# Latent attention: up-projection in two 128-row products per head pair, partner rows by a VectorE shuffle, another step order

## The reference

```python
c_q = _rmsnorm(x @ w_q_down.T, q_norm_w)                       # 192
q = (c_q @ w_q_up.T).reshape(b, t, H, 128 + 64)
q_nope, q_rope = q[..., :128], q[..., 128:]
kv = x @ w_kv_down.T
c_kv, k_rope_raw = kv[..., :64], kv[..., 64:]                   # one key rope for all heads
q_rope, k_rope = _apply_rope(q_rope, ...), _apply_rope(k_rope_raw, ...)
kv_up = (_rmsnorm(c_kv, kv_norm_w) @ w_kv_up.T).reshape(b, t, H, 128 + 128)
scores = q_full . k_full / sqrt(192), causal mask, softmax, @ v, @ w_o.T
```

## Time and profile before

| what | value |
|---|---|
| runs, us | 4121.14, 4110.23, 4107.7 (median 4110.23) |
| profiled execution, span | 4117.8 us |
| TensorE (PE) busy | 3583.7 us, 87% of the span |
| VectorE (DVE) busy | 3057.9 us, 74% |
| ScalarE (ACT) busy | 1939.7 us, 47% |
| GpSimd (POOL) busy | 1167.6 us, 28% |
| mean granted TensorE clock | 0.928 of 2.4 GHz |

### The profile page before, as it was taken

The page is one execution under the profiler, slowest core; times in us unless marked ns, Lnnn a source line. Parts: engine busy times, 40 slices in busy tenths (PEclk is TensorE's granted clock), DMA queues, the critical chain, the costliest instruction groups (busy, mean ns, idle before and its releaser), DMA issues. The chain is left out here.

```text
span 4117.8 us, 65960 instructions
## 1 busy us (share of the span) xinstructions
PE 3583.7 (87%) x23747; PEld 2223.2 (54%) x23762; DVE 3057.9 (74%) x6508; ACT 1939.7 (47%) x4746; POOL 1167.6 (28%) x1208
## 2 busy tenths in 40 slices
PE   7799999998981777879999979888999999997885
PEld 3466666665661345645455545465655656564543
DVE  7788988988658675543455657868988898885678
ACT  4466666665532333311333324435656656563445
POOL 2533213334302000000111122114656555553210
PEclk9899999999995888889899988999999999997877
DMA  2222222222200100020000000022212211221000
GB/s 70 65 66 67 60 62 65 66 56 56 61 14 31 34 1 24 2 76 1 22 1 1 1 31 2 27 92 83 77 68 77 72 72 72 67 79 63 2 1 21
DMA packets 240594, 185.94 MB, mean 45 GB/s; under 512 B 117648, under 2 KB 216592, under 8 KB 239184
## 3 DMA queue, kind: packets, MB, share of 16 engines
q1 hardware_dynamic: 240272, 181.73, 14.7%
HBM read 166.45 MB, written 15.20 MB: 44 GB/s over the span
## 5 line engine op out<-in xcount | busy, mean ns | idle before, releaser
L310 PE MATMUL ps<-xT,min 128*128 128x512 f32 (+1 forms) x1072 | 503.0, 614 | 30.7 <-DVE macc L3349 30.3
L3349 DVE SCALAR_TENSOR_TENSOR macc<-ps,mcw,macc 128x508 f32<-128x508 f32 (+2 forms) x408 | 302.1, 741 | 81.2 <-ACT macc L3276 71.3
L3431 POOL TENSOR_TENSOR mSQ<-mSQ,mtn 128x512 f32<-128x512 f32 x128 | 240.2, 1877 | 362.1 <-ACT mtn L3301 362.0
L310 PEld LDWEIGHTS ps<-xT,min 128*128 128x128 f32 (+1 forms) x1072 | 191.9, 191 | 250.6 <-issue 204.3
L3424 POOL TENSOR_TENSOR mE<-mE,mCB 128x1024 f32<-128x1024 f32 x128 | 302.3, 2362 | 44.5 <-DVE mE L3359 26.5
L3359 DVE TENSOR_TENSOR_SCAN mE<-mE,mid 128x1024 f32<-128x1024 f32 x128 | 296.9, 2319 | 0.0
L3209 PE MATMUL ps<-mwo,macc 128*128 128x256 f32 x1024 | 244.5, 382 | 5.4 <-DVE macc L3366 5.3
L2937 ACT ACTIVATE hE<-ps 128x512 f32<-128x512 f32 x256 | 139.0, 595 | 223.5 <-PE ps L2899 223.5
L2351 POOL TENSOR_TENSOR lP<-lP,lm 128x512 f32<-128x512 f32 x64 | 66.6, 1041 | 574.5 <-DVE lm L2324 574.5
L3297 ACT ACTIVATE mtn<-ps,mcol 128x64 f32<-128x64 f32 x1024 | 222.9, 334 | 2.9 <-PE ps L3188 2.8
L826 POOL TENSOR_TENSOR dTB<-did,dNB 128x1024 f32<-128x1024 f32 (+1 forms) x10 | 28.7, 2869 | 662.6 <-DMA dNB<-d_N 598.4
(11 more groups left out here) (581 smaller groups left out, 8470.9 us busy)
## 6 DMA issues: line engine op xcount, KB each, us to landing
mE<-m_decay SPq DMA_DIRECT2D x128, 512.0 KB, 3.6
dwk<-in_L_attn_Wk SPq DMA_DIRECT2D x64, 128.0 KB, 2.3
dwq<-in_L_attn_Wq SPq DMA_DIRECT2D x64, 128.0 KB, 2.4
dwv<-in_L_attn_Wv SPq DMA_DIRECT2D x64, 128.0 KB, 2.4
dwg<-in_L_attn_Wg SPq DMA_DIRECT2D x64, 128.0 KB, 2.4
dwo<-in_L_attn_Wo SPq DMA_DIRECT2D x64, 128.0 KB, 2.6
min<-in_m_in SPq DMA_DIRECT2D x2, 4096.0 KB, 18.5
d_N<-dNT SPq DMA_DIRECT2D x256, 16.0 KB, 1.5
```

The lines of the kernel that those rows point to most:

```text
L310: t = pe.matmul(out, w[:, j, :], self.c.xT[:, j, blk(g, 512)], start=j == 0, stop=j == 1)
L3349: x = dve.scalar_tensor_tensor(out=acc[:, :, 3 - j:T], in0=p[:, :, 0:T - 3 + j], scalar=self.cw[:, i, j:j + 1], in1=acc[:, :, 3 - j:T], op ...
L3431: pool.tensor_tensor(self.SQ[g % 2][:, :], self.SQ[g % 2][:, :], self.tn[s][:, :], ALU.add).then_inc(*self.sqa.up)
```

## The change

Per pair there is one step `q` in place of `sw` and two `q`: the swapped rotary rows of both heads into bank 2 (matrix qr, what sw_ was) and the latent rows of both heads, second head first, into bank 3 (matrix ql, which step `a` fills). The plain rotary rows are not multiplied any more; VectorE takes them from the swapped ones in bank 2, by a shuffle that exchanges neighbouring partitions (into QC), multiplies bank 2 with the sines (into QS), later QC with the cosines (step `rope`), and adds both into QA for each head. The second chunk of c_q, 64 rows, stands twice in CQ, on partitions 0-63 and 64-127 (CN has 64 columns more for it, one more scaling per 128 tokens; tr1 turns 128 rows), so that the 64-row product of bank 3 reads other rows of the array than that of bank 2. The reciprocals are a step of their own (`rc`), and the order of the list changes. M2 is written by `o` alone. Two loads of the q matrix go, two of a column of norm weights come.

```diff
-            for step, u, e in (("sw", a, 0), ("t", c, 0), ("s", b, 0), ("q", a, 0), ("t", c, 1), ("s", b, 1), ("q", a, 1), ("o", c, 0),
-                               ("acc", d, 0), ("close", d, 0), ("stats", t - 4, 0), ("rsqrt", t - 5, 0), ("scale", t - 6, 0)):
+            for step, u, e in (("s", b, 0), ("rc", c, 1), ("t", c, 0), ("q", a, 0), ("s", b, 1), ("rc", b, 0), ("t", c, 1), ("rope", a, 0),
+                               ("acc", d, 0), ("o", c, 0), ("close", d, 0), ("stats", t - 4, 0), ("rsqrt", t - 5, 0), ("scale", t - 6, 0)):
...
-    TURNS = ((0, 128), (128, 64), (192, 128))
+    TURNS = ((0, 128), (128, 128), (256, 128))
+    PARTNER = [p ^ 1 for p in range(32)]
...
-            elif step in ("sw", "q"):
-                n, b = (0, 2) if step == "sw" else (e + 1, 3)
-                pe.wait_ge(*room[b])
...
-                for i, K in enumerate((128, 64)):
-                    w = self.sw_[0:K, i, blk(pr)] if n == 0 else self.q[0:K, i, 2 * pr + e, :]
-                    t = pe.matmul(bank(b), w, self.CQ[gs][0:K, i, :], start=i == 0, stop=i == 1)
-                t.then_inc(*self.up.up)
-                room[b] = self.m2.at(u + 1) if n == 0 else self.qa.at(2 * u + e + 1)
+                pe.wait_ge(*room[2])
+                pe.matmul(bank(2), self.qr[:, 0, blk(pr)], self.CQ[gs][:, 0, :], start=True, stop=False)
+                pe.wait_ge(*room[3])
+                pe.matmul(bank(3), self.ql[:, 0, pr, :], self.CQ[gs][:, 0, :], start=True, stop=False)
+                pe.matmul(bank(2), self.qr[0:64, 1, blk(pr)], self.CQ[gs][0:64, 1, :], start=False, stop=True)
+                pe.matmul(bank(3), self.ql[64:128, 1, pr, :], self.CQ[gs][64:128, 1, :], start=False, stop=True).then_inc(*self.up.up)
+                room[2], room[3] = self.m2.at(u + 1), self.lat.at(2 * u + 2)
             elif step == "s":
...
                 pe.wait_ge(*self.qa.at(2 * u + e + 1))
+                pe.wait_ge(*self.lat.at(2 * u + e + 1))
...
-                    for r in (192, 256):
+                dve.tensor_scalar(CN[:, b, 192:256], p[:, 256 * j + 128:256 * j + 192], sn[:, b:b + 1], None, ALU.mult)
+                    for r in (256, 320):
...
-            elif step == "sw":
-                dve.wait_ge(*self.up.at(3 * u + 1))
...
-                dve.tensor_tensor(g4(self.M2[s][:, :]), g4(bank(2)), bc(self.cs[:, 1, :], 4), ALU.mult).then_inc(*self.m2.up)
-            elif step == "q":
...
-                then(dve.tensor_tensor(g4(self.QA[s][rot, e, :]), g4(bank(3)[rot, :]), bc(self.cs[rot, 0, :], 4), ALU.mult))
-                dve.wait_ge(*self.lat.at(2 * u + e + 1))
-                dve.tensor_tensor(self.QA[s][rot, e, :], self.QA[s][rot, e, :], self.M2[s][rot, :], ALU.add).then_inc(*self.qa.up)
+            elif step == "q":
+                dve.wait_ge(*self.up.at(u + 1))
+                if u:
+                    dve.wait_ge(*self.qa.at(2 * u))
+                dve.stream_shuffle(self.QC[:, :], bank(2), self.PARTNER).then_inc(*self.swapped.up)
+                dve.tensor_tensor(g4(self.QS[:, :]), g4(bank(2)), bc(self.cs[:, 1, :], 4), ALU.mult).then_inc(*self.m2.up)
+            elif step == "rope":
+                dve.wait_ge(*self.swapped.at(u + 1))
+                dve.tensor_tensor(g4(self.QC[:, :]), g4(self.QC[:, :]), bc(self.cs[:, 0, :], 4), ALU.mult).then_inc(*self.turned.up)
...
+                for e in range(2):
+                    rot = blk(e, 64)
+                    dve.tensor_tensor(self.QA[s][rot, e, :], self.QC[rot, :], self.QS[rot, :], ALU.add).then_inc(*self.qa.up)
...
+            elif step == "rc":
+                me = self.m[s][:, e, :]
                 dve.wait_ge(*self.ex.at(2 * u + e + 1))
```

More of the change, by code:

```diff
@@ L2109, in tensor @@
                 n, i = divmod(g, 2)
[L2110 removed]
+                rows = slice(64 * i, 128)
                 pe.wait_ge(*room[g])
                 for h in range(8):
[L2113 removed]
+                    t = pe.matmul(bank(g)[rows, blk(h, 64)], self.qT[:, 8 * n + h, 128 * i:192 if i else 128], self.kvT[:, 8 * n + h, 0, :],
                                   start=True, stop=True)
@@ L2184, in tensor @@
                     for x in range(2):
-                        t = pe.matmul(bank(5)[blk(x, 64), blk(j)], self.CN[gs][:, j, 192:256], self.PT[s][:, x, blk(j)], start=True, stop=True)
+                        t = pe.matmul(bank(5)[blk(x, 64), blk(j)], self.CN[gs][:, j, 256:320], self.PT[s][:, x, blk(j)], start=True, stop=True)
                 t.then_inc(*self.o.up)
@@ L2213, in scalar @@
                 n, i = divmod(g, 2)
-                rows = 64 if i else 128
+                rows = slice(64 * i, 128)
                 act.wait_ge(*self.am.at(g + 1))
-                act.copy(self.q[0:rows, i, 8 * n:8 * n + 8, :].rearrange("p (q e) n -> p q (e n)", e=2)[:, :, 64:192],
-                         bank(g)[0:rows, :].rearrange("p (q n) -> p q n", n=128)).then_inc(*self.ac.up)
+                to = self.ql[rows, i, 4 * n:4 * n + 4, :]
+                of = bank(g)[rows, :].rearrange("p (q e n) -> p q e n", e=2, n=64)
+                act.copy(to[:, :, 64:128], of[:, :, 0, :])
+                act.copy(to[:, :, 0:64], of[:, :, 1, :]).then_inc(*self.ac.up)
             elif step == "b":
@@ L2243, in scalar @@
                 if i < 2:
-                    x = act.activation(self.CQ[gs][0:n, i, :], bank(6)[0:n, :], ACT.Copy, scale=self.nw[0:n, i:i + 1])
+                    x = act.activation(self.CQ[gs][0:n, i, :], bank(6)[0:n, :], ACT.Copy, scale=self.nw1[:, 1:2] if i else self.nw[:, 0:1])
                 else:
@@ L2249, in scalar @@
             elif step == "q":
-                lat = slice(64 - 64 * e, 128 - 64 * e)
-                act.wait_ge(*self.up.at(3 * u + e + 2))
+                act.wait_ge(*self.up.at(u + 1))
                 if u >= 4:
-                    act.wait_ge(*self.sc.at(2 * u - 8 + e + 1))
-                act.copy(self.QA[s][lat, e, :], bank(3)[lat, :]).then_inc(*self.lat.up)
+                    act.wait_ge(*self.sc.at(2 * u - 6))
+                for e in range(2):
+                    lat = slice(64 - 64 * e, 128 - 64 * e)
+                    act.copy(self.QA[s][lat, e, :], bank(3)[lat, :]).then_inc(*self.lat.up)
             elif step == "s":
@@ L2347, in gpsimd @@
         for step, g, u, e in self.order():
-            if step == "s":
+            if step == "rc":
                 pool.wait_ge(*self.rc.at(2 * u + e + 1))
```

44 lines of the change are left out of this document (21 added, 23 removed).

## The result

| | before | after |
|---|---|---|
| median, us (lowest to highest, 4 runs each) | 4108.97 (4097.44 to 4121.14) | 3992.29 (3980.23 to 3998.22) |
| ratio, 95% interval | | 0.9704 (0.9678 to 0.9731) |
| span of the profiled execution, us | 4117.8 | 3996.4 |
| the stage, us | 508.1 | 385.5 |
| everything else of the span, us | 3609.7 | 3610.9 |

The change makes the kernel faster by 116.7 us in the medians and by 121.4 in the profiled executions. It takes 122.6 us less; the rest of the program is the same within 1.2.

What follows compares the result with a forecast made beforehand. TensorE bounded the pairs (12.2 of 13.13 us); afterwards a TensorE-VectorE ring. Start to 1987.3, thirty periods of 9.17 (275.1) and shared 50 give 2312.4 against 2430.2; with tail -1.5, 119 us less: 3991, range 3970 to 4030.

Steps and rivals of the forecast that it cites:

- The products: TensorE per head pair: packed 64-row passes take two slots of 0.57, q 2.85, total work 8.90 us instead of 12.2.
- Rival A: The 64-row passes of q don't pack: the ring grows by 1.14 us per pair, 36 in all, so 4027; chance 0.15.
- three slots: 64-row passes in strict program order, only the middle two side by side: 0.57 x 32 = 18 us more, 4009.
- The ring: Loop through TensorE and VectorE: sums read at 4.39, next scores at 9.17; period 9.17 us, TensorE waiting 0.27.
- Rival B: VectorE's shuffle and permutation load are dearer: 0.7 us more per pair in the ring, 22 in all, 4013; chance 0.13.
- The collision with GpSimd: VectorE's SBUF cosine product overlaps GpSimd's normalisation of P: about 0.7 us lost per microsecond of overlap, so 0.69 + 0.40.
- dn: Down-projection step, three times in the loop: scores 8.7 us late plus 2.5 for the lowered clock, 11.2 each.
- Shared steps: Steps inside the loop (dn, tr, r, close, stats, rsqrt, scale): 16.7 us together, three times, 50.
- The start: Stage's beginning: 0.94 us later from four more scalings; second pair 10.5 us at the lower clock, reaching 1987.3.
- The tail: After the last pair's scores: the same chain with one small reordering, 1.5 us less.
- Rival C: VectorE's chain keeps TensorE at the lower clock in the loop: 250 us more, 4240, slower than before; chance 0.04.
- Rival D: Stalls are cheaper: period 8.97 without permutation cost and no clock loss after dn, -6 - 8, 3977; chance 0.05.

Runs made afterwards that it cites:

- cosine-early kernel: The changed kernel with the cosine product directly behind the sine product in step q instead of in step rope: 3987.25 us, stage 382.6.
- the last experiment: The changed kernel with VectorE's part of dn behind t(c,0) and the sixteen dn scalings moved to ScalarE: 3978.1 us, stage 370.0.

## Why the prediction held, step by step

The stage lost 122.6 us, forecast 119. That the medians lie within 1.3 us of the 3991 is closer than single runs of one kernel (3980.23 to 3998.22) allow, and so partly luck; the stage and its parts are the test.

**The products: right, a little cheap.** The 64-row passes start together in banks 2 and 3, and a slot of two is 0.53 (2252.57 to 2253.10) where I had 0.57; q is 2.87 for 2.85. With t at 0.43 for 0.50, TensorE's work is 8.82 us (9.15 less 0.33) for 8.90. Rival A, unpacked, is excluded by the rows and by the kernel that has it so, whose stage is 18.1 us longer and not 36. The Trainium skill (TensorE: Matmul & The Clock Gate, Packing small matmuls) has matmuls start and end strictly in program order; here the passes in the order high, low, high, low run as two pairs, so the three slots that I had worked out from it did not come. The rows don't show in which order the two of a pair start.

**The ring: right in place and length, two of its terms wrong.** Sums readable to the next scores took 4.73 us (2253.75 to 2258.48), forecast 4.78. The permutation load costs 0.01, not 0.17; the shuffle 0.63 from start to start, not 0.60; the cosine product 1.27 to the first add, not 1.09, being 1.14 long and 0.13 more until the add sees it. The errors cancel: the period is 9.15 for 9.17. Rival B (0.7 more in the chain) falls with the rows of lQC, and doubling the shuffle shows that such a price would have come through in plain pairs, yet only about half of it over the stage, so B's 22 us were too many (an estimate from that run).

**The collision with GpSimd: right in size, wrong in kind.** I had taken 0.7 us lost for each microsecond of overlap, from one row. Rows at other distances show something else: an instruction of VectorE with two inputs in SBUF that starts while GpSimd's runs stands still at first, and then takes its full 0.69. Counted to the recorded end of GpSimd's instruction (2257.06) the product would take 0.59 + 0.69 = 1.28 us; it took 1.14, 0.14 less. The same 0.14 to 0.15 comes out of the add before (started 0.57 behind, 1.02 long), of 28 others of these adds (0.68 behind, 0.91 long), of one product after (0.80 behind, 0.79 long) and of the adds of the cosine-early kernel: a block that ends 0.14 before GpSimd's recorded end fits them all, a rate doesn't. It works the other way round too, as the new products in the old order show, where the product starts 0.16 us ahead of GpSimd:

```profile
2291.98 0.66 DVE L2315 TENSOR_TENSOR lQC<-lQC,lcs 128x512 f32<-128x512 f32 x1
...
2292.14 1.40 POOL L2360 TENSOR_TENSOR lP<-lP,lm 128x512 f32<-128x512 f32 x1 [2.77 <-DVE lm L2333]
```

There the product is undisturbed and GpSimd's takes 1.40 for 1.04. The Trainium skill (SBUF — State Buffer, SBUF: two separate sides) describes an exclusive lock under which the later instruction fully blocks. These rows agree, in both directions; why the recorded end comes 0.14 us after the release, no run shows.

**dn: right, and by the right path.** TensorE around it, timeline of the kernel after:

```profile
2069.62 3.72 PE L316 MATMUL ps<-ldn,xT 128*128 128x256 f32 x16
...
2083.34 0.61 PE L2167 MATMUL ps<-identb,neg 128*128 128x512 bf16 x1 [5.68 <-ACT lP L2264]
2083.74 1.91 PE L2171 MATMUL ps<-lKK,lQA 128*128 128x128 f32 x8
...
2090.66 1.05 PE L2171 MATMUL ps<-lKK,lQA 128*128 128x128 f32 x8
```

From dn's start the next pair's scores are 21.0 us away (2090.66); forecast 20.9, 18.4 and 2.5 for the clock. TensorE stands for 5.68 us, and the scores behind the hole take 1.91 for 1.05. dn costs about 11 us each time: it was the largest thing left, as the last experiment shows.

**Shared steps: right in sum.** A tr pair with nothing else in it took 9.31 (0.16 over the plain one, forecast 0.23), the two r pairs 10.64 each (3.0 together over plain ones, forecast 3.1), and close, stats, rsqrt and scale 2.1 together (forecast 1.7). From the second pair's first scores (1985.09) to the last pair's (2306.32) it is 321.2 us. The forecast has 325.1 there (275.1 + 50), but counts in it the first dn's product, which lies ahead of 1985.09; less its 3.45 it is 321.6.

**The start: 4 us too pessimistic.** The first q came 31.51 us after step a, 0.29 later than before and not 0.94. The four more scalings delay the first turn by 0.78 (0.19 each, not 0.24), but the first r product behind the turns took 2.96 us for 3.52 before: part of it ran at the lower clock in both, less of it after (granted clock 0.64 in it for 0.53). And I gave the second pair the lower clock (10.5, dn still to come); with 3.45 of dn in it, it took 10.34. The granted clock was 0.79 from 1972 to 1980 and 1.00 from there to 1990. That step a itself began 1.64 us earlier is the stage ahead, not the change.

**The tail: 1.1 us too optimistic, and wrong in sign at an equal clock.** 16.4 us from the last pair's scores to the end of acc (before 16.8); I had taken 1.5 off. The granted clock there was 1.00 after and 0.90 before. In the three kernels whose end ran at 0.91 it took 18.5 us from the last pair's mask on, where the kernel before took 17.0: the new tail is the longer one, and a higher clock hid it.

**Rival C** (the ring keeps TensorE at the lower clock) falls: 1.00 in plain pairs, where it waits 0.33 in 9.15. But the mechanism is there: behind dn (0.62 from 1990 to 2000), and all over the new products in the old order (0.91 in the mean). Rival D's cheap permutation came true, its free clock didn't.

One bound of mine was too narrow: that no other stage's span would move by over 2 us. From before to after the rest moved by 1.2 in sum, but between the executions of this case it moves by up to 18.6, so the bound could have called a right prediction wrong.

## What to carry to other kernels

Lay the loop out as a ring before counting on a cut in one engine's work: the products alone gave 33.5 us, the order alone 42.5, both 122.6, because each alone left the other's bound standing. Once the plain pairs are such a ring, with TensorE at work for 8.82 of 9.15 us, the gain lies in the pairs that break it: find the engine that is almost without a gap there (VectorE, 13.23 us of work behind dn) and move work to one that isn't; moving it later on the same engine gives little. Read a bound from the starts of instructions and not from a busy share: with 9.95 of 10.00 and 8.90 of 9.04 us busy, TensorE was still waiting for VectorE in every pair. Judge edits of a few microseconds by the length of their stage in the trace, when the rest of the program varies by more, and look at the granted clock of its parts.

## What the runs showed of the hardware

- Two 64-row passes on rows 0-63 and 64-127, into different banks, start within 0.01 us of each other and cost 0.53 us per two; on the same rows four of them took 1.91 us.
- A partner shuffle of 128x512 fp32 out of PSUM takes 0.73 us (0.63 from start to start), the load of its permutation 0.014, and a plain copy in its place leaves the period as it is.
- Of an instruction of VectorE with two SBUF inputs and one of GpSimd that overlap, the later one stands still: VectorE's ends 0.69 us (its own length) after a point 0.14 to 0.15 us ahead of GpSimd's recorded end, whether it started 0.41 us behind it (1.17 us long), 0.45 (1.14), 0.57 (1.02), 0.68 (0.91) or 0.80 (0.79); started 0.16 us ahead, it takes 0.66, and GpSimd's 1.40 for 1.04.
- The holes behind dn cost clock as well: granted 0.80 in the pair with the 5.68 us hole (0.72 in the first such pair), 0.90 with a hole of 4.57 (dn's part taken behind the reduce), and 1.00 where ScalarE did the scalings.
